# A two-layer decoder on one core: batch 0 stacked ahead, the second half projected inside the first attention

## The reference

```python
x = x + attention_rope(ln(x), wq, wk, wv)            # 16 heads of 8, full softmax
x = x + aft(ln(x), ctx, ctx)                         # sigmoid(Q) * (E @ (exp(K-maxK) * V)) / (E @ exp(K-maxK))
x = x + moe_linear(ln(x), w_gate, w_in, w_out)       # 8 experts, top 2
x = x + linear_attention(ln(x))                      # softmax features, biases
x = x + masked_cross_attention(ln(x), ctx, mask)     # causal, 16 heads of 8
x = x + four_rounds_of_moe_gelu(ln(x))               # 4 experts, top 2
```

## Time and profile before

| | |
|---|---|
| median of three runs | 524.55 us (521.68 to 524.81) |
| the profiled execution | 520.7 us, of which its span, first to last instruction, 519.0 us |
| PE busy / weight loads | 452.1 us (87%) / 347.5 us (67%) |
| DVE, ACT, POOL busy | 347.9, 305.4, 131.6 us |
| granted PE clock, mean | 0.935 of full speed |
| chain that ended last, by engine | PE 63%, DVE 15%, issue 9%, ACT 6%, POOL 3%, DMA 2%, SP's queue 2% |

### The profile page before, as it was taken

One profiled execution on the slowest core, in us unless ns is written; L12 is line 12 of the kernel. 1 busy time (PEld: TensorE's weight loads), 2 busy tenths in 40 slices (PEclk: granted clock), 3 DMA queues, 4 the chain that ended last, 5 costly groups with the idle time before them and its releaser, 6 DMA issues.

```text
span 519.0 us, 8370 instructions
## 1 busy us (share of the span) xinstructions
PE 452.1 (87%) x2660; PEld 347.5 (67%) x2660; DVE 347.9 (67%) x942; ACT 305.4 (59%) x600; POOL 131.6 (25%) x193
## 2 busy tenths in 40 slices
PE   3779999977983997579998966999999999999995
PEld 2448777756631785448777755878787787878783
DVE  4477767777488555546768836768585867777653
ACT  2447676542354442035666536788887778788781
POOL 6070000222165000214654430021221222212121
PEclk9978999999995898857999977999999999999999
DMA  8911111000400000011111000120102020120201
GB/s 295 362 57 30 32 30 32 11 1 1 163 1 0 1 1 1 0 24 36 35 32 24 20 0 21 63 83 1 81 0 81 1 81 11 71 71 12 83 1 40
DMA packets 13954, 24.51 MB, mean 47 GB/s; under 512 B 4160, under 2 KB 11456, under 8 KB 12256
## 3 DMA queue, kind: packets, MB, share of 16 engines
q1 hardware_dynamic: 13488, 23.23, 13.6%
q10 hardware_dynamic: 432, 0.85, 0.4%
HBM read 19.29 MB, written 0.59 MB: 38 GB/s over the span
## 4 chain that ended last, share of the span: by engine, by line
PE 63%; DVE 15%; issue 9%; ACT 6%; POOL 3%; DMA 2%; SPq 2%; ACTq 0%; POOLq 0%; DVEq 0%
PE ps L1223 6%; PE ps L1537 5%; PE ps L1539 4%; PE ps L1538 4%; PE ps L1268 4%; PE ps L1550 4%; PE ps L1549 4%; PE ps L1548 4%; PE ps L1235 3%; POOL xnT L452 2%; DVE masked L814 2%; PE ps L1456 2%; SPq L298 2%; DVE big L931 2%; PE ps L1280 1%
## 5 line engine op out<-in xcount | busy, mean ns | idle before, releaser
L1071 DVE TENSOR_TENSOR bigr<-ps,bigr 128x512 fp32r<-128x512 f32 x128 | 86.3, 689 | 54.4 <-ACT ps L682 54.4
L681 ACT ACTIVATE bigr<-ps,b 128x512 fp32r<-128x512 f32 x128 | 89.8, 701 | 36.7 <-PE ps L1539 36.7
L546 ACT ACTIVATE big<-ps 128x512 f32<-128x512 f32 (+1 forms) x128 | 68.7, 548 | 51.0 <-PE ps L1235 49.0
L682 ACT ACTIVATE ps<-ps,b 128x512 f32<-128x512 f32 x128 | 86.6, 677 | 0.0
L452 POOL TENSOR_TENSOR xnT<-xnT,big 128x512 f32<-128x512 f32 x32 | 41.4, 1295 | 155.6 <-DVE big L1079 155.6
L1223 PE MATMUL ps<-bigr,qk 128*128 128x256 f32 (+1 forms) x224 | 53.6, 322 | 3.7 <-DVE nmax L821 1.5
L1537 PE MATMUL ps<-k1hi,w1hi 128*128 128x512 f32 x128 | 53.5, 418 | 3.5 <-ACT xnT L472 2.9
L821 DVE TENSOR_REDUCE nmax<-ps 128x2 f32<-128x512 f32 x64 | 42.7, 688 | 16.2 <-PE ps L1223 15.4
L1235 PE MATMUL ps<-qk,bigr 128*128 128x256 f32 (+1 forms) x256 | 51.0, 284 | 1.0 <-ACT big L546 0.7
L1539 PE MATMUL ps<-k1lo,w1hi 128*128 128x512 f32 x128 | 51.3, 401 | 0.0
L1538 PE MATMUL ps<-k1hi,w1lo 128*128 128x512 f32 x128 | 51.3, 401 | 0.0
(11 more groups left out here) (191 smaller groups left out, 806.1 us busy)
## 6 DMA issues: line engine op xcount, KB each, us to landing
big<-gates SPq DMA_DIRECT2D x8, 1024.0 KB, 4.8
bigr<-qk SPq DMA_DIRECT2D x128, 32.0 KB, 1.9
wi<-in_wi SPq DMA_DIRECT2D x1, 2048.0 KB, 8.2
wo<-in_wo SPq DMA_DIRECT2D x1, 2048.0 KB, 12.5
big<-in_sel SPq DMA_DIRECT2D x1, 1024.0 KB, 8.4
wo<-in_w SPq DMA_DIRECT2D x1, 1024.0 KB, 4.7
wi<-in_w SPq DMA_DIRECT2D x1, 1024.0 KB, 6.8
x<-in_x SPq DMA_DIRECT2D x1, 512.0 KB, 5.2
```

The source lines that it names most:

```text
L546: act.activation(prob[:, h % 8, c], ps[:, 2 + h % 2, c], ACT.Exp, scale=DH ** -0.5).then_inc(s(L + "_exp"), 1)
L681: act.activation(ghi[:, u % 2, c, :], ps[:, c, :], ACT.Gelu_apprx_tanh, bias=b1[:, u % E1, c:c + 1])
L682: act.activation(ps[:, c, :], ps[:, c, :], ACT.Gelu_apprx_tanh, bias=b1[:, u % E1, c:c + 1]).then_inc(s("ff1_gel"), 1)
L1071: v.tensor_tensor(glo[:, u % 2, c, :], ps[:, c, :], ghi[:, u % 2, c, :].bitcast(f32), ALU.subtract).then_inc(s("ff1_glo"), 1)
```

## The change

All of it lies in the opening and the first self-attention. The first stacks wait for batch 0 alone (256 columns) instead of the first half. `batch_ready` names a semaphore value for batches 0, 1 and 2. PE does context tiles 0 and 1, the transposes of the first half, tile 2, the first half's projections, the second transposes, tile 3 and the first half's values; the second half's four projections, its values and context tiles 4 to 7 are put into slots 0 to 14 of batch 0, with banks 2, 3 and 7. ACT copies the second half's raw projections out and POOL (no longer DVE) multiplies them by cosine and sine; batch 1's add and remainder go to POOL as well, and the selector cast. The context maximum becomes one reduction inside batch 1, its subtractions POOL work in batch 1, the exponentials ACT work in batch 2. A context tile is read out by two operations instead of three. The expert weights are loaded in eight parts of 512 KB between the key copies of batches 1 and 2. ACT issues the identity first.

```diff
--- SP
+            def expert_weights(part):
+                e = slice(2 * (part // 2), 2 * (part // 2) + 2)
+                dst, src = ((wi0, "wi0"), (wo0, "wo0"))[part % 2]
+                load("ff0", dst[:, e, :, :], w[src][:, e, :, :])
-            load("ff0", wi0[:, :, :, :], w["wi0"])
-            load("ff0", wo0[:, :, :, :], w["wo0"])
...
+                    between(n)                       # at the end of each group's four copies
-            padded_keys("at0")
+            padded_keys("at0", lambda n: expert_weights(n - G) if G <= n < G + E0 else None)
--- POOL
+            pool.wait_ge(s("ld_sel"), 32)
+            pool.tensor_copy(selr[:, :, :, :, :], sel).then_inc(s("sel_r"), 1)
             for n, a in enumerate((1, 0)):
                 pool.wait_ge(s("at0_rot"), 4 + 2 * (n + 1))
-                pool.tensor_tensor(rot1[1][:, a, :], rot1[1][:, a, :], rot2[1][:, a, :], ALU.add)...
...
+                pool.tensor_tensor(rot1[0][:, a, T:2 * T], rot1[0][:, a, T:2 * T], rot2[0][:, a, T:2 * T], ALU.add
+                                   ).then_inc(s("at0_sum1"), 1)
+            for n, a in enumerate((1, 0)):
                 pool.wait_ge(s("at0_hi"), 2 + n + 1)
+                pool.tensor_tensor(qlo[:, a, T:2 * T], rot1[0][:, a, T:2 * T], qhi[:, a, T:2 * T].bitcast(f32),
+                                   ALU.subtract).then_inc(s("at0_lo1"), 1)
+            pool.wait_ge(s("at0_vev"), 1)
+            for g in range(G):
+                head_values("at0", v_tok, 0, g)
+            pool.wait_ge(s("ld_rope"), 16)
+            for n, a in enumerate((1, 0)):
+                for part, rows in enumerate((rot1[1], rot2[1])):
+                    pool.wait_ge(s("at0_raw"), 2 * n + part + 1)
...
+                    own.mark(pool.tensor_tensor(halves, halves, rope[:, part:part + 1, :].broadcast_to([P, 2, T]), ALU.mult))
+                own.wait()
+                pool.tensor_tensor(rot1[1][:, a, :], rot1[1][:, a, :], rot2[1][:, a, :], ALU.add)...
+            for n, a in enumerate((1, 0)):
+                pool.wait_ge(s("at0_hi"), 4 + n + 1)
                 pool.tensor_tensor(qlo[:, a, HALF:2 * HALF], ...)
-            for b in range(B):
+            for b in range(1, B):
                 for g in range(G):
                     head_values("at0", v_tok, b, g)
+                    if b == 1 and g >= G - TPB:
+                        context_differences(g - (G - TPB))
+                    if b == 2 and g == 0:
...
+                        pool.tensor_tensor(expbT[:, :, :], wbiasT[:, :, :], wbiasT[:, :, :], ALU.subtract)...
--- ACT
-            for name, dst, src in (("ctx", ctxT[:, :], "ctxT"), ("ctx", wctx[:, :, :], "wctx"), ("ident", ident[:, :], "ident")):
+            for name, dst, src in (("ident", ident[:, :], "ident"), ("ctx", ctxT[:, :], "ctxT"), ("ctx", wctx[:, :, :], "wctx")):
...
-                    act.activation(ek[:, jt, b, :], ps[:, 4 + n % 2, 0:D], ACT.Copy)
-                    act.activation(ekv[:, jt, b, :], ps[:, 4 + n % 2, D:2 * D], ACT.Copy)
+                act.activation(ek_ekv[:, :, jt, b, :], ps[:, bank, 0:2 * D].rearrange("p (a d) -> p a d", a=2), ACT.Copy)
...
+            def raw_projection(n):
+                k = (2, 3, 0, 1)[n]
+                act.wait_ge(s("at0_qk"), 4 + n + 1)
+                act.activation((rot1[1], rot2[1])[k % 2][:, k // 2, :], ps[:, LATE_BANKS[n], :], ACT.Copy).then_inc(s("at0_raw"), 1)
...
+            context(0, 4)
+            context(1, 5)
+            evacuate_xnT("at0", 0)
+            context(2, 4)
+            rotated((s("at0_sum"), 1), 1, slice(0, T), rot1[0][:, 1, 0:T])
+            evacuate_xnT("at0", 1)
+            rotated((s("at0_sum"), 2), 0, slice(0, T), rot1[0][:, 0, 0:T])
+            context(3, 5)
+            self_values(0, 4)
+            evacuate_first_stacks("at0")
+            for n, a in enumerate((1, 0)):
+                rotated((s("at0_sum1"), n + 1), a, slice(T, 2 * T), rot1[0][:, a, T:2 * T])
...
+                    if not causal and b == 2 and k == 3:
+                        context_keys()
+                    if not causal and b == 2 and k == 14:
+                        context_bias()
...
-            attention("at0", False)
+            attention("at0", False, {0: lambda: raw_projection(0), 1: lambda: raw_projection(1),
+                                     2: lambda: raw_projection(2), 4: lambda: raw_projection(3), 6: late_values,
+                                     9: lambda: context(4, 7), 11: lambda: context(5, 7), 12: rotated_late,
+                                     13: lambda: context(6, 7), 15: lambda: context(7, 7)})
--- DVE
-            own.mark(v.tensor_copy(selr[:, :, :, :, :], sel))
...
+            def context_maxima():
+                dve.wait_ge(s("ctx_ev"), NT)
+                v.tensor_reduce(ctx_max[:, :, :], ek.rearrange("p k b d -> p k d b"), AX.X, ALU.max).then_inc(s("ctx_mx"), 1)
...
+            rotate(0, 1)                             # rotate(b, a): 256 columns
             rotated_sum(0, 1)
+            rotate(0, 0)
             rotated_rest(0, 1)
             rotated_sum(1, 0)
+            rotate(1, 1)
             rotated_rest(1, 0)
+            rotate(1, 0)
...
+                    if b == 1 and not causal and k == 6:
+                        context_maxima()
--- PE
+            context(0, 4)
+            context(1, 5)
             pe.wait_ge(s("ld_ident"), 16)
+            transpose_xn("at0", 0)
+            pe.wait_ge(s("ctx_ev"), 1)
+            context(2, 4)
...
+            for n, k in enumerate((2, 3, 0, 1)):
+                rotary_projection(0, n, k)
+            transpose_xn("at0", 1)
+            pe.wait_ge(s("ctx_ev"), 2)
+            context(3, 5)
+            pe.wait_ge(s("ctx_ev"), 3)
+            self_values(0, 4)
...
+            def late_projections(k):
+                if k == 0:
+                    rotary_projection(1, 0, LATE_BANKS[0])       # LATE_BANKS = (2, 3, 7, 2)
+                elif k == 1:
+                    rotary_projection(1, 1, LATE_BANKS[1])
+                    pe.wait_ge(s("at0_stkev"), 2)
+                    rotary_projection(1, 2, LATE_BANKS[2])
+                elif k == 3:
+                    pe.wait_ge(s("at0_raw"), 1)
+                    rotary_projection(1, 3, LATE_BANKS[3])
+                elif k == 5:
+                    pe.wait_ge(s("at0_raw"), 3)
+                    self_values(1, 7)
+                elif k == 6:
+                    pe.wait_ge(s("at0_raw"), 4)
+            def late_context(n):
+                if n == 4:
+                    pe.wait_ge(s("at0_vev"), 2)
+                else:
+                    pe.wait_ge(s("ctx_ev"), n)
+                context(n, 7)
+            pe.wait_ge(s("sel_r"), 1)
...
+            pe.wait_ge(s("at0_vev"), 1)
+            pe.wait_ge(s("ctx_ev"), NT // 2)
+            attention("at0", False, qhi[:, 1, :], qlo[:, 1, :],
+                      {0: (s("at0_lo"), 2), 1: (s("at0_lo1"), 2), 2: (s("at0_lo1"), 4)},
+                      lambda: pe.wait_ge(s("at0_rot"), 8), aft_sums,
+                      early={0: ..., 1: ..., 3: ..., 5: ..., 6: ...,       # late_projections(slot)
+                             8: lambda: late_context(4), 10: lambda: late_context(5),
+                             12: lambda: late_context(6), 14: lambda: late_context(7)})
```

More of the change, by code:

```diff
@@ L24 @@
 FIRST_BANKS = (6, 7, 4, 5)
+LATE_BANKS = (2, 3, 7, 2)
 LN_EPS, Z_EPS = 1e-5, 1e-6
@@ new lines, in _ @@
+            pool.wait_ge(s("at0_vev"), 1)
[5 more added lines that the diff above has]
+                    pool.wait_ge(s("at0_raw"), 2 * n + part + 1)
+                    halves = rows[:, a, :].rearrange("p (b t) -> p b t", b=2)
+                    own.mark(pool.tensor_tensor(halves, halves, rope[:, part:part + 1, :].broadcast_to([P, 2, T]),
+                                                ALU.mult))
+                own.wait()
+                pool.tensor_tensor(rot1[1][:, a, :], rot1[1][:, a, :], rot2[1][:, a, :], ALU.add).then_inc(s("at0_sum1"), 1)
@@ L512, in _ @@
[L512 to L521, removed]
@@ L1136, in transpose_xn, with context @@
                 last.then_inc(s("ln_xT"), 1)
[L1138 to L1152 removed]
+            def context(n, bank):
+                pe.matmul(ps[:, bank, 0:3 * D], ctxT[:, n * P:n * P + P], wctx[:, 0:3, :], start=True, stop=True
+                          ).then_inc(s("ctx_pe"), 1)
@@ new lines, in rotary_projection, with self_values @@
+            def rotary_projection(hf, n, bank):
+                pe.matmul(ps[:, bank, :], w0[:, (2, 3, 0, 1)[n], :], xnT[:, hf * HALF:hf * HALF + HALF],
+                          start=True, stop=True).then_inc(s("at0_qk"), 1)
+            def self_values(hf, bank):
+                for n in range(4):
+                    tile = 4 * hf + n
+                    last = pe.matmul(ps[:, bank, n * D:n * D + D], xnT[:, tile * P:tile * P + P], w0[:, 4, :],
+                                     start=True, stop=True)
+                last.then_inc(s("at0_v"), 1)
```

(22 more changed lines are left out.)

146 lines of the change are left out of this document (68 added, 78 removed).

## The result

| | before | after |
|---|---|---|
| median of the runs taken together | 524.68 us (4 runs, 521.68 to 524.86) | 517.0 us (4 runs, 516.14 to 517.57) |
| ratio after / before | | 0.9865, 95% interval 0.9826 to 0.9905 |
| the profiled execution (its span) | 520.7 us (519.0) | 516.49 us (514.8) |
| granted PE clock, mean | 0.935 | 0.945 |

What follows compares the result with a forecast made beforehand. PE was taken to bound batches 1 to 3, latency the opening and batch 0. Gaining 8.0 us there, less 0.5 and 0.6 later, gives 6.9: 524.55 - 6.9 = 517.6 us, range 512.7 to 523.5.

Steps and rivals of the forecast that it cites:

- Context weights: Opening: third in ACT's queue instead of second, they land between 7.8 and 9.8 us, taken as 8.5.
- second rival: A late start: context weights land at 9.8, 1.3 late; first two projections at half clock, 1.4 late; gain 4.2; chance 0.10.
- The path from there: Opening: transposes at 11.2, projections from 12.75, second remainder done at 18.95, first stacks at about 19.4 us instead of 27.86.
- The selector cast: Opening: moved from DVE to POOL, it costs 1.8 to 6.4 us, hidden under the rotation up to 19.4: nothing.
- DVE's subtraction beside POOL's add: Opening, before the first stacks: DVE's last subtraction overlaps POOL's add for batch 1; bounds 0 and 1.1 us, taken at 0.
- Slots 0 to 7: Batch 0: 10.4 us from first stack to slot 8, set by SP's key copies; PE's 7.1 us of work fits under it.
- third rival: PE's clock falls to 0.50 near 21 us through batch 0; batch 1 at 51.1, kernel 5.1 us slower; chance 0.10.
- Slots 8 to 15: Batch 0 with four context tiles added: 9.3 us at full clock, bounds 8.9 and 12.0; batch 1 starts at 39.1.
- The context maximum, 0.5: Batch 1, ahead of DVE's seventh maximum: the reduction takes 1.3 us and PE loses 0.5, bounds 0 and 1.3.
- both later terms: Batches 1 and 2: PE's losses of 0.5 us to the context maximum and 0.6 to ACT's two exponentials, together 1.1.
- Batch 2's exponentials: Batch 2: ACT does two exponentials, 1.06 and about 0.6 us; the scores two heads on wait 0.6, bounds 0 and 1.7.
- The sum: Whole kernel: 8.0 - 0.5 - 0.6 = 6.9 us gained, against the median 524.55, so 517.6 us.

## Why the prediction came true, and where it was wrong

- *Context weights: 8.5, bounds 7.8 to 9.8.* **Wrong, and outside its bounds: 10.26.** I let the small load ahead count little. The order of the three loads is the cause: with the context first, PE starts at 8.10 and the stacks come at 18.77. It is the first half of the second rival, at 1.8 us late instead of 1.3; its other half, projections at half clock, did not come.
- *The path from there.* Right. Transposes 2.7 us behind the first context product, as forecast; projections to second remainder 5.8 (6.2); the values read out come last, then the stacks, 6.5 behind the projections (6.65). The selector cast took 1.89 of its 1.8 to 6.4 us and hid.
- *DVE's subtraction beside POOL's add, taken at 0.* Right: 0.41 us at 20.25, with POOL's adds from 20.41; below, POOL's two adds in the kernel before:

```profile
20.25 0.41 DVE L818 TENSOR_TENSOR bigr<-big,bigr 128x256 fp32r<-128x256 f32 x1
...
20.41 0.83 POOL L362 TENSOR_TENSOR big<-big 128x256 f32<-128x256 f32 x1 [6.70 <-DVE big L807]
...
21.40 0.73 POOL L362 TENSOR_TENSOR big<-big 128x256 f32<-128x256 f32 x1 [0.16 <-DVE big L807]
```

```profile
26.95 1.65 POOL L361 TENSOR_TENSOR xn<-xn,big 128x512 f32<-128x512 f32 x1 [16.85 <-DVE big L758]
...
28.75 1.38 POOL L361 TENSOR_TENSOR xn<-xn,big 128x512 f32<-128x512 f32 x1
```

  The Trainium skill ("GPSIMD Engine Reference", Specifications) has the two engines collide when DVE reads two SBUF inputs; these rows agree, and they show which of the two pays. Where DVE began first, its subtractions kept their time (0.68 at 26.79, 0.41 here) and POOL's add took longer than the one behind it (1.65 against 1.38, 0.83 against 0.73). Where POOL's add had begun first, at 28.75, DVE's maximum at 28.92 took 1.50 instead of 0.42. The prediction read the subtraction at 26.79 as one without a collision; its 0 came true because DVE began first again.
- *Slots 0 to 7, 10.4 us set by SP.* Right in size (10.37), but not in its reserve. I gave PE 7.1 us of work; it was busy 8.49 of 8.72, because a projection between other weights takes about 1.0 instead of 0.86, and four of the eight pairs of maxima at 32 rows about 0.43 instead of 0.24. With little slack left, most of what a fall of the clock costs shows: 13.2 and 13.1 us in the two profiles that have one. The third rival is thus half true: the fall comes in two of the four profiles, but it lasts 6.9 us and ends before slot 8, so batch 1 starts 2.3 us later, not the 12 (51.1 against 39.1) by which the kernel would have become slower.
- *Slots 8 to 15, 9.3 us (8.9 to 12.0).* 9.98 to 10.01 in all four profiles: inside the bounds, 0.7 over the value. The term is PE's own: 7.5 us without the tiles and 2.5 with them.
- *The context maximum, 0.5.* **Wrong: the worst term.** I priced 1024 inputs at twice the 0.69 of a 512-wide maximum, 1.3; it took 1.95, and PE waited 1.13 for it where I had 0.5. With both later terms I had 1.1 for batches 1 to 3; they take 1.5 us more than before in the one profile without a fall of the clock there, and 3.1 to 3.5 in the three with it. The bound of 1.3 held for the wait, but did not ask what a fall of the clock behind it would cost: the prediction looked for such holes in batch 0 only.
- *Batch 2's exponentials, 0.6.* A third of it: from the values in slot 12 of batch 1 to those in slot 0 of batch 3 PE takes 0.2 us more than before (23.07 against 22.88), nearly all of it beside the bias's exponential.
- *The sum.* Forecast 6.9; the runs give 5.3 and the profiles 2.7. It was set against the median of three runs, 524.55, where 85 runs have a mean of 523.2. A gain too large from a base too high gave 517.6 beside a mean of 517.9: two errors that cancel by luck, and a range wide enough to hold what the single terms did not.

## What to carry to other kernels

When a stage that waits on latency is filled with moved work, look for where the next hole opens, in the stages behind it too: here batches 1 to 3 gave back 1.5 to 3.5 of the 5.6 us by which batch 1 started earlier, most of it at one long DVE operation. Price a load by what stands ahead of it in its queue, however small that is, and put first the one that the chain waits for. And set a sum against many runs of the kernel before: single executions of the kernel before lie up to 7 us apart here, more than the whole gain.

## What the runs showed of the hardware

- A 64 KB load ahead of 512 and 256 KB in one queue moved the landing of the last from 7.77 to 10.26 us, though its issue came only 0.49 later. What the other 2.0 us are (the loads that SP issues meanwhile, or the small load itself) was not tried. The Trainium skill ("DMA: Bandwidth & Descriptors", Queues, rings and completion order) says that each DMA engine takes the descriptors of a queue in order; here the loads landed in the order of their issue.
- A DVE maximum of four strided inputs to an output took 1.95 us for 1024 inputs and 1.06 for 512, against 0.69 for 512 inputs from PSUM to two outputs.
- The clock falls at different places in different executions of one kernel: after the change, in batch 0 at 23 us in two profiles of four and in batch 1 at 52 to 54 us in three. The Trainium skill ("TensorE: Matmul & The Clock Gate", Part 1) says that the point at which the clock rises in a kernel's first matmuls varies from run to run; the falls in these profiles vary likewise. The same hole of 1.1 us in PE's work had a fall behind it in three of the seven profiles that have the hole, so what it costs on the mean is seen only over several profiles.
- Where a DVE operation with two SBUF inputs and an add of POOL overlapped, the one that began second took longer, in all eight profiles of the two kernels: POOL's adds 1.65 instead of 1.38 us and 0.83 instead of 0.73, DVE's maximum 1.50 instead of 0.42.
